# Splitting the expert-weight load between the SyncE and the GpSimd DMA queue, with the scratch store moved behind the next loads

## What is computed

```
xn  = layernorm(x)
q   = rope(xn @ Wq + bq);  kv = (xn @ Wdown + bdown) @ Wup + bup;  k, v = split(kv)
att = softmax(einsum('bthd,btgd->bthg', q, rope(k)) / 8)     # over the 16 heads g of one token
a   = einsum('bthg,btgd->bthd', att, v) @ Wout + bout
top1 = argmax(softmax(xn @ router_w.T + router_b)); weight = its probability
f   = (xn @ expert_w[top1].T + expert_b[top1]) * weight       # 8 experts of 1024 x 1024
out = x + a + f
```

## Time and profile before

| what | value |
|---|---|
| time, median of 2 runs | 2725.86 us (2722.8 to 2728.92) |
| the profiled execution's own time | 2722.11 us |
| its span, slowest core (core 2) | 2720.6 us |
| spans of the 8 cores | 2702.7 to 2720.6 us |
| busy share of the span: PE, DVE, ACT, POOL | 70%, 32%, 21%, 4% |
| chain that ended last: PE, DMA, DVE, ACT | 57%, 18%, 11%, 5% |
| of it DMA y_f<-exw (the expert loads) | 5% |
| mean DMA rate over the span | 135 GB/s |

### The profile page before, as it was taken

The page is one execution under the profiler, slowest core; times in us unless marked ns, Lnnn a source line. Parts: engine busy times, 40 slices in busy tenths (PEclk is TensorE's granted clock), DMA queues, the critical chain, the costliest instruction groups (busy, mean ns, idle before and its releaser), DMA issues.

```text
span 2720.6 us, 39164 instructions; the slowest of 8 cores (2702.7 to 2720.6 us)
## 1 busy us (share of the span) xinstructions
PE 1893.0 (70%) x16622; PEld 1539.8 (57%) x16622; DVE 859.7 (32%) x1041; ACT 568.5 (21%) x834; POOL 106.6 (4%) x210
## 2 busy tenths in 40 slices
PE   0111158778787878686878878787878687777877
PEld 0111147666565756575756666575757575666655
DVE  2111133242424242423333242424141433324241
ACT  0122241121303031313121120303031312213030
POOL 0000000000000000000000000000000000000000
PEclk9965578788787979797988788798979697888879
DMA  5356524234251425252524334152426252433413
GB/s 148 131 195 227 207 97 178 101 128 152 93 186 63 167 82 187 62 217 62 186 93 161 118 125 155 63 194 84 157 68 211 62 202 78 154 125 119 145 63 139
DMA packets 60800, 366.47 MB, mean 135 GB/s; under 512 B 7107, under 2 KB 8131, under 8 KB 26580
## 3 DMA queue, kind: packets, MB, share of 16 engines
q1 hardware_dynamic: 31828, 179.41, 20.0%
q0 software_dynamic: 28800, 184.56, 18.2%
HBM read 330.39 MB, written 33.55 MB: 134 GB/s over the span
## 4 chain that ended last, share of the span: by engine, by line
PE 57%; DMA 18%; DVE 11%; ACT 5%; issue 4%; DVEq 3%; ACTq 2%; SPq 1%; POOL 0%; POOLq 0%
PE psb L824 28%; DMA exbuf<-exscratch 10%; PE psb L734 5%; DMA y_f<-exw 5%; PE psb L876 5%; PE psa L726 4%; PE psb L773 2%; PE psa L757 2%; PE psa L889 2%; DVE exbuf L301 1%; DVEq L218 1%; ACTq L511 1%; DVE pav L465 1%; DVE mrep L391 1%; DVE y_f L490 1%
## 5 line engine op out<-in xcount | busy, mean ns | idle before, releaser
L824 PE MATMUL psb<-xe,exbuf 128*128 128x256 bf16 x8192 | 976.9, 285 | 133.3 <-DVE xe L474 69.1
L824 PEld LDWEIGHTS psb<-xe,exbuf 128*128 128x128 bf16 x8192 | 829.8, 102 | 283.5 <-issue 157.3
L474 DVE TENSOR_TENSOR xe<-xnf,mrep 128x2048 bf16<-128x2048 bf16 x96 | 116.2, 1224 | 457.7 <-PE psb L824 453.9
L700 PE MATMUL psa<-idbf,exbuf 128*128 128x128 bf16 x512 | 49.0, 278 | 198.8 <-DVE exbuf L301 195.1
L726 PE MATMUL psa<-rT_sb,xnf 128*128 128x8 f32 x512 | 111.5, 361 | 85.1 <-DVEq L218 85.1
L773 PE MATMUL psb<-lat,wup_sb 128*128 128x256 bf16 x1024 | 146.3, 297 | 34.5 <-ACTq L511 27.5
L726 PEld LDWEIGHTS psa<-rT_sb,xnf 128*128 128x128 f32 x512 | 110.4, 332 | 88.6 <-issue 88.6
L700 PEld LDWEIGHTS psa<-idbf,exbuf 128*128 128x128 bf16 x512 | 45.6, 130 | 202.1 <-issue 201.7
L490 DVE COPY y_f<-psb 128x2048 f32<-128x2048 f32 x16 | 36.7, 2291 | 360.0 <-PE psb L881 360.0
L773 PEld LDWEIGHTS psb<-lat,wup_sb 128*128 128x128 bf16 x1024 | 101.6, 106 | 82.2 <-issue 63.2
L734 PE MATMUL psb<-xnf,wq_sb 128*128 128x256 bf16 x1024 | 147.3, 318 | 0.0
(11 more groups left out here) (123 smaller groups left out, 1627.2 us busy)
## 6 DMA issues: line engine op xcount, KB each, us to landing
exbuf<-exscratch SPq DMA_DIRECT2D x128, 1024.0 KB, 5.6
exbuf<-exscratch POOLq DMA_DIRECT2D x128, 1024.0 KB, 8.7
y_f<-exw SPq DMA_DIRECT2D x64, 512.0 KB
x_t<-x POOLq DMA_DIRECT2D x32, 512.0 KB, 6.3
exscratch<-exbuf POOLq DMA_DIRECT2D x8, 2048.0 KB, 10.0
out<-outsb POOLq DMA_DIRECT2D x32, 512.0 KB, 8.6
y_f<-wq SPq DMA_DIRECT2D x8, 512.0 KB
y_f<-wo SPq DMA_DIRECT2D x8, 512.0 KB
```

The source lines that it names most:

```text
L474: vector.tensor_tensor(out=re(xe[:, 2048 * (ex_i % 2):2048 * (ex_i % 2) + 2048], "p (cc t) -> p cc t", t=256), in0=src0, in1=m1.broadcast_ ...
L700: li = tensor.transpose(out=psa_bf[:, 1024 * (kd % 4) + 128 * jo: 1024 * (kd % 4) + 128 * (jo + 1)], in_=exbuf[:, 1024 * jo + 128 * kd:102 ...
L824: li = tensor.matmul(out=pout(m), lhsT=exbuf[:, eb + 1024 * k + 128 * m: eb + 1024 * k + 128 * (m + 1)], rhs=xe[:, xb + 256 * k:xb + 256 * ...
```

## The change

The loads of the right half of the staging tile go from SyncE to GpSimd, with a semaphore of their own, `swg`; VectorE waits for both semaphores. GpSimd waits for the same count of `smV` as SyncE does before each half. The store of expert ex-1 now stands in GpSimd's program behind its four half loads of expert ex; the store of expert 7 follows at the end.

```diff
+        swg = e(nc.semaphore("swg"))
@@ gpsimd
+            VCB = P0_V - 2 - 32
             for ex in range(8):
-                gpsimd.wait_ge(smS, 1 + 8 * (ex + 1))
+                for sr in range(4):
+                    gpsimd.wait_ge(smV, VCB + 4 * ex + sr)
+                    gdma(wstage[:, 1024:2048],
+                         exw_d[ex, 128 * (2 * sr + 1):128 * (2 * sr + 2), :], swg)
                 if ex > 0:
-                    gpsimd.wait_ge(sexp, 16 * ex)
-                gdma(exs_d[ex], exbuf[:, 8192:16384], sexp)
+                    gpsimd.wait_ge(smS, 1 + 8 * ex)
+                    if ex > 1:
+                        gpsimd.wait_ge(sexp, 16 * (ex - 1))
+                    gdma(exs_d[ex - 1], exbuf[:, 8192:16384], sexp)
+            gpsimd.wait_ge(smS, 1 + 8 * 8)
+            gpsimd.wait_ge(sexp, 16 * 7)
+            gdma(exs_d[7], exbuf[:, 8192:16384], sexp)
@@ vector
+            gcount = 0
             for ex in range(8):
                 for sr in range(4):
-                    wcount += 2
+                    wcount += 1
+                    gcount += 1
                     vector.wait_ge(sw, 16 * wcount)
+                    vector.wait_ge(swg, 16 * gcount)
@@ sync
                     dma(wstage[:, 0:1024], exw_d[ex, 128 * 2 * sr:128 * (2 * sr + 1), :])
-                    dma(wstage[:, 1024:2048],
-                        exw_d[ex, 128 * (2 * sr + 1):128 * (2 * sr + 2), :])
```

## The result

| | before | after |
|---|---|---|
| median time | 2727.54 us (29 runs) | 2735.49 us (30 runs) |
| ratio | | 1.0033, 95% interval 1.0023 to 1.0043 |
| spans of the 8 cores in the profiled execution | 2702.7 to 2720.6 us | 2712.4 to 2735.1 us |

So the change costs 9 us (6 to 12), 0.33%. The time lies 8.5 us above the forecast 2727 and within the range. It is "within 2%", as forecast, but the loss is clear of zero, and my sum had only 1.3 us of it.

What follows compares the result with a forecast made beforehand. The 103 to 350 us expert stretch was taken as bound by waiting, mainly VectorE's casts for loads. Seven waits at 0.19 us (+1.3) plus a free split (0) gave 2723.4 on the profiled execution, 2727 as median; range 2706 to 2752.

Steps and rivals of the forecast that it cites:

- my sum: Expert stage: seven store waits at 0.19 us each, +1.3 us, plus 18 pitch changes of 0, giving +1.3 us in all.
- the landing of the store: Moved 2 MB expert store, issue to landing: taken as 10.1 us, today's median beside loads, from a range of 9.8 to 11.5.
- the new place looks like today's: Moved store: a 1 MB load issued 1.3 us ahead and another while it runs, so today's 10.1 us landing was kept.
- third cast's end to ScalarE's first copy: Each expert change: store issue 1.3, landing 10.1 and wake-up 0.05 make 11.45 us, a new ScalarE wait of 3.8.
- two free pitches: Casts of slabs 1 and 2, no longer beside the store: each pitch falls to 6.24 us, from 8.35 and 8.71.
- A's own range: Main case, chance 0.70: store delay and freed slabs cancel, 2727 us; landing, issue and split uncertainties give about 2715 to 2743.
- The seventh wait: Expert stage's two ends: first expert without wait, last one's after its fourth cast, together counted as one of seven at 0.19 us.
- First copy to next cast: Expert change, ScalarE's first copy to VectorE's first cast of the next expert: taken as 5.53 us, as in the kernel before.
- The split, d = 0: Half loads on GpSimd: change of a free slab's pitch, counted 18 times, taken as 0; bounds -0.3 and +4.3 us.
- rival C: GpSimd's half loads get no engine for a fixed 3 us: small price 2749 us, chance 0.14; large price 2804, chance 0.04.
- Hidden slab: Next expert's first slab, loaded beside the store: lands at 13 to 14 us, wanted at 17, so hidden with 3 us margin.
- B: Rival, a gain: moved store lands in 7.6 us as when alone, and the half loads overlap; -23 us, 2703; chance 0.12.

Runs made afterwards that it cites:

- e1: Changed kernel, but the store issued behind GpSimd's half load of slab 1, about its old place, leaving the load split alone: ratio to before 0.9987.
- e2: Kernel before, SyncE still loading both halves, but each expert's store issued only after the next expert's third cast: ratio to before 1.0046.
- e8: Changed kernel with the store one slab earlier, behind GpSimd's half load of slab 2 instead of slab 3: ratio to before 0.9993.
- e3: Changed kernel with two alternating output buffers, so ScalarE's first copy waits only for the store of two experts ago: ratio to before 0.9992.
- e11: Changed kernel with each expert's first slab, from the third expert on, loaded only after the store in flight has landed: ratio to before 1.0014.
- e9: e6 with each slab's right half loaded by GpSimd and the store behind the half load of slab 2: ratio to before 0.9787.
- e6: Kernel before with three staging tiles for expert slabs, all loads by SyncE, and two output buffers, store at its old moment: ratio to before 0.9690.

## Why the prediction was right, and which term it mis-sized

**The mechanism held.** The store's delay became a wait of ScalarE, seven times; the two slabs after it ran free; the two nearly cancelled. e1 and e2 put the parts apart: from the first cast to the stage end the split alone costs 2.6 us, which the time doesn't show, the late store alone 10.9, and the changed kernel 12.5. e8 shows that it is a threshold and e3 that it is the wait.

**The mis-sized term** is the landing of the store, "I take 10.1". Here are the steps of the sum beside the means over all cores and the experts 1 to 6:

| step | forecast | measured |
|---|---|---|
| third cast's end to the store's issue | 1.3 | 1.10 |
| issue to landing | 10.1 | 11.74 (10.5 to 13.9) |
| third cast's end to ScalarE's first copy | 11.45 | 12.91 |
| first copy to the next expert's first cast | 5.53 | 5.78 |
| two free pitches | 6.24 each | 6.27 and 6.30 |
| an expert | 30.70 | 32.51 |
| an expert before | 30.51 | 30.36 |

The 1.64 us in the landing have two sources. First, 10.1 is the median of core 2 alone, the slowest core, whose page is printed. Over all 8 cores the stores of the kernel before took 10.9 us for the same experts (9.6 to 12.2), and core 2's, at 10.3, were among the fastest; only core 3 had 10.2. The slowest core of an execution isn't typical for each of its terms; views of the other cores would have shown it. Second, "the new place looks like today's" is not quite so: the moved store took 0.9 longer than that. Without the load issued while it runs it takes 10.2 (e11), so that load is enough to explain the difference; why it costs more here than the one that in the kernel before runs into the store's end was not tried. The upper end that I gave the landing, 11.5, was passed by the mean itself. An expert is 1.8 us dearer than forecast; the landing is 1.64 of it, the earlier issue took 0.2 back, and the next paragraphs have the rest.

**The range.** The parts of A's own range add up to 2719 to 2748 us, not to the 2715 to 2743 that the forecast has. The measured 2735.5 lies in both and in the full range, but it got there with a landing beyond its own bounds and with some luck outside the stage, as the paragraph on the seventh wait shows.

**The seventh wait.** "The first expert has no such wait, and the last one's wait falls after its fourth cast; together they are one of the seven" holds in count, not in price. From the second expert's third cast to the eighth's there are six periods, and each cost 2.15 us more than before, 12.9 in all. Behind them, the last fourth pitch took 1.3 us more, and from the last cast to the stage end it is 15.8 us instead of 13.6, so +2.2. Ahead of them, the way from the first expert's third cast to the second's fell by 4.1, because its slabs ran free and no store was waited for. So the two ends together returned 0.6 us, where I had charged them like one more period. 12.9 + 3.5 - 4.1 = +12.3 us; the stage end moved by 12.9, the rest being earlier than the third cast. The mean span of the cores moved by 9.3 and the time by 9. The remaining 3.5 us are in the main loop of the two profiled executions, 2359.1 against 2355.5, which is within the scatter over the kernels. That the time lies no further from the forecast is owed to this scatter.

**First copy to next cast, +0.25.** I took 5.53 as fixed. It holds transposes that TensorE makes in step with ScalarE, and a slower clock lengthens them. Busy time by stretch, first the changed kernel, then the kernel before, each the last groups of one expert. The columns are those of the earlier trace rows; the third number from the right is the granted clock:

```profile
195.67:200.40 4.73, 4.67 (x40) 3.84 (x40) 0.00 (x0) 4.73 (x6) 0.00 (x0) 0.50 0.02 7
```

```profile
196.50:199.10 2.60, 1.82 (x24) 1.39 (x24) 0.00 (x1) 2.60 (x4) 0.00 (x0) 1.00 0.00 0
```

In the expert shown of the kernel before, TensorE worked through the groups with no pause over 0.4 us and was granted 2.4 GHz for the last three, 0.61 us each. In the one of the changed kernel it makes three groups, stands still for 4.4 us until the store lands and ScalarE copies, and makes the other five at 1.2 GHz, 0.94 us each. The last one is on the path to VectorE's cast. It isn't so every time. Over the 8 cores and six changes of expert, 48 cases, the last group took 0.61 us in all of the kernel before, and first copy to next cast was 5.53 or 5.54. In the changed kernel the last group still took 0.61 or 0.62 us in 15 cases, with 5.53 or 5.54 from copy to cast. In the other 33 it took up to 1.01, with up to 5.94. The 0.25 is the mean of the two kinds.

**The split, d = 0.** The free pitches grew by 0.03 and 0.06 us and the first expert's 0.1 us; the changed kernel alone can't say whether that is the split or the execution. The reading behind it, and against rival C, can be seen in two stretches of the changed kernel's queues, GpSimd's half having been issued at 110.77: 110.3 to 112.9 us, then 112.9 to 114.9.

```profile
q1 hardware_dynamic: 99, 0.41, 57.7%
```

```profile
q0 software_dynamic: 144, 0.52, 64.1%
q1 hardware_dynamic: 45, 0.12, 14.9%
```

q0 is silent for 2.1 us where it was silent for 3.15, with 0.41 MB of q1 moved where it was 0.84. With nothing queued ahead, at the last store, q0's first packet came 1.1 us after the issue, on every core and in both kernels. So the silence grows with what SyncE has queued ahead; it is queueing and no fixed delay of 3 us. C, at either price, is out: the half loads landed at 4.3 us. The Trainium skill ("DMA: Bandwidth & Descriptors", Queues, rings and completion order) has an engine take turns between queues by packets; this trace disagrees: q0's first packet came only behind 0.41 MB of q1's here, and behind 0.84 MB before the change. The Trainium skill's rule on the same page (Rules for kernel authors), that spreading DMAs over issuing engines brings no bandwidth, agrees with e1, and e9 gained none over e6 either, 247 against 289 GB/s.

**Hidden slab.** I had the slab beside the store landing 3 us before it is wanted. In the changed kernel GpSimd's half of it landed 3.5 us before the first cast on average and 1.7 at the least, and all seven first casts on every core were released by TensorE, none by the load, so it stayed hidden. In e3, where the transposes come sooner, that cover is gone, and last to first is 8.63 instead of 8.15 us.

**B** needed stores below 9 us. The fastest of the waited-for ones took 9.5.

## What to carry to other kernels

- A transfer that nobody waits for can be moved only as far as its cover reaches, and the cover is to be counted against its slow landings, over all cores, not against the median of the core that is printed: here some 5 us of the landing stuck out over a cover of 7.65, seven times, and ate more than the freed loads gave.
- If a stage is bound by loading and consuming one buffer in turns, another queue or another order of the same DMAs has little to give: nothing measurable, and at most some 20 us, here. Look for idle memory and put more loads in flight: three staging tiles gave 3.1%, and 4.3% with all the weights.
- Be wary of putting loads on a queue that also carries a large store: in e9 half loads of 512 KB behind a 2 MB store landed after 13.8 to 16.9 us.

## What the runs showed of the hardware that I had not expected

- A 2 MB store is lengthened by a 1 MB load issued 5.6 to 7.6 us after it: 11.5 us to landing with it, 10.2 without (e11).
- A wait in the middle of TensorE's work can cost once more afterwards: in the expert shown, transposes at 0.94 us a group of 8 instead of 0.61, at a granted clock of 0.50 instead of 1.00. In 33 of 48 cases the last group was slowed; the mean cost was 0.25 us a wait.
- GpSimd's queue moved its first packet 1.1 us after the issue with nothing queued by SyncE, 2.1 with 512 KB queued and 3.15 with 1 MB in the stretches shown.
- With all loads on SyncE's queue and the stores on GpSimd's, the 16 DMA engines were 90% busy at 289 GB/s with all 8 cores at work (e6), where the same transfers in turns had 196.
